# Local transformer: second norm centred on TensorE, PSUM banks and engine orders laid out anew; mixture of experts: routing in groups, gates spread by DMA

## The reference, cut to what matters

```
def attn_layer(x, Wqkv, qs, ksc, Wo):
    q, k, v = jnp.split(x @ Wqkv, 3, -1)
    q = l2norm(q) * qs          # l2norm(t) = t / max(norm(t), 1e-12)
    k = l2norm(k) * ksc
    q, k = rotary with scale (q * cos * scale + rotate_half(q) * sin * scale; k with 1/scale)
    out = local_attention(q, k, v)      # softmax over this window and the one before
    return out @ Wo

def ffn_layer(x, g, bln, W1, b1, W2, b2):
    xn = (x - mean) / jnp.sqrt(var + 1e-05) * g + bln
    a, gate = jnp.split(xn @ W1 + b1, 2, -1)
    return a * jax.nn.gelu(gate, approximate=False) @ W2 + b2

for i in range(6):
    x = attn_layer(shift_tokens(x), ...) + x
    x = ffn_layer(shift_tokens(x), ...) + x
```

```
logits = xf @ router_w + router_b
gates = softmax over the two largest logits, 0 elsewhere     # first index wins a tie
out = sum_e gates[:, e] * (silu(xf @ w1[e]) * (xf @ w3[e]) @ w2[e]) + the same, ungated, of 2 shared experts
```

## Time and profile before

| | |
|---|---|
| median of 3 runs | 6157.06 us |
| the profiled execution | 6155.58 us, its span 6153.5 us |
| PE busy | 5219.1 us, 85% of the span |
| VectorE busy | 4318.1 us, 70% |
| ScalarE busy | 3341.5 us, 54% |
| GpSimd busy | 2611.7 us, 42% |
| mean granted TensorE clock | 0.937 of full speed |
| local transformer | about 1460 to 5295 us of the span |
| mixture of experts | about 5694 to 5963 us of the span |

### The profile page before, as it was taken

One profiled execution on the slowest core, in us unless ns is written; L12 is line 12 of the kernel. 1 busy time (PEld: TensorE's weight loads), 2 busy tenths in 40 slices (PEclk: granted clock), 3 DMA queues, 4 the chain that ended last, 5 costly groups with the idle time before them and its releaser, 6 DMA issues. The chain is left out here.

```text
span 6153.5 us, 131444 instructions
## 1 busy us (share of the span) xinstructions
PE 5219.1 (85%) x50625; PEld 3447.1 (56%) x50817; DVE 4318.1 (70%) x6996; ACT 3341.5 (54%) x5697; POOL 2611.7 (42%) x1602
## 2 busy tenths in 40 slices
...
GB/s 70 55 55 55 18 0 6 2 2 26 11 10 10 28 10 10 10 25 15 10 10 25 15 10 10 25 15 10 10 25 13 11 11 10 11 2 2 7 14 17
DMA packets 74175, 105.08 MB, mean 17 GB/s; under 512 B 21576, under 2 KB 52504, under 8 KB 71072
## 3 DMA queue, kind: packets, MB, share of 16 engines
...
HBM read 61.19 MB, written 2.36 MB: 10 GB/s over the span
## 5 line engine op out<-in xcount | busy, mean ns | idle before, releaser
L2180 POOL TENSOR_TENSOR lt_qk<-lt_qk,lt_rot 128x1024 f32<-128x1024 f32 x384 | 905.2, 2357 | 512.2 <-DVE lt_rot L2534 512.2
L2190 POOL TENSOR_TENSOR lt_prob<-lt_prob,lt_total 128x1024 f32<-128x1024 f32 x192 | 365.3, 1902 | 1238.0 <-DVE lt_total L2560 1231.9
L2229 PE MATMUL lt_ps<-lt_w_qk,lt_xs 128*128 128x512 f32 x1536 | 759.9, 618 | 53.4 <-issue 31.8
L2185 POOL TENSOR_TENSOR lt_qk<-lt_qk,lt_rnorm 128x1024 f32<-128x1024 f32 x384 | 727.9, 1907 | 57.1 <-ACT lt_rnorm L2408 49.5
L2280 PE MATMUL lt_ps<-lt_z,lt_fold 128*128 128x256 f32 x3072 | 678.8, 379 | 1.2 <-ACT lt_z L2436 1.2
L2401 ACT ACTIVATE lt_sq<-lt_ps 128x1024 f32<-128x1024 f32 x384 | 393.4, 1025 | 480.8 <-PE lt_ps L2229 472.4
L2280 PEld LDWEIGHTS lt_ps<-lt_z,lt_fold 128*128 128x128 f32 x3072 | 583.6, 190 | 121.4 <-ACT lt_z L2436 24.3
L2531 DVE TENSOR_TENSOR lt_qk<-lt_ps,lt_table 128x1024 f32<-128x1024 f32 x384 | 466.1, 1214 | 156.2 <-ACT lt_sq L2401 151.9
L2534 DVE TENSOR_TENSOR lt_rot<-lt_ps,lt_table 128x512 f32<-128x512 f32 x768 | 488.9, 675 | 0.0
L2541 DVE TENSOR_REDUCE lt_norm<-lt_sq 128x16 f32<-128x1024 f32 x384 | 463.8, 1208 | 0.0
L2550 DVE TENSOR_REDUCE lt_nmax<-lt_ps 128x16 f32<-128x1024 f32 x192 | 235.1, 1225 | 308.7 <-PE lt_ps L2248 308.4
...
## 6 DMA issues: line engine op xcount, KB each, us to landing
mb_bs<-mb_rows SPq DMA_DIRECT2D x16, 1536.0 KB, 7.6
lt_xw<-lt_xw SPq DMA_DIRECT2D x192, 128.0 KB
mb_bs<-mb_rows SPq DMA_DIRECT2D x16, 512.0 KB, 4.3
...
lt_wvT<-in_L_wvT SPq DMA_DIRECT2D x6, 512.0 KB, 7.2
lt_wo<-in_L_ffn_Wo SPq DMA_DIRECT2D x6, 512.0 KB, 8.4
```

The lines of the kernel that those rows point to most:

```text
L2180: pool.tensor_tensor(qk[:, u, :, :], qk[:, u, :, :], rot[:, u % 2, :, :], ALU.add).then_inc(sg["added"], 1)
L2185: pool.tensor_tensor(qk[:, u, :, :], qk[:, u, :, :], rnorm[:, u, :, :].to_broadcast([P, H, DH]), ALU.mult).then_inc(sg["qk"], 1)
L2229: last = pe.matmul(AT[u][:, 512 * k:512 * k + 512], xs[:, m.j, c:c + P], w_qk[:, a, 512 * k:512 * k + 512], start=True, stop=True)
```

## The change

In the local transformer: `floor` leaves DVE; its work is done on ACT by a Relu of the sum less 1e-24, and the Ln's bias adds it back. The mean is no longer taken and subtracted: one product with `center_w` (identity less 1/128) writes the centred values to PSUM, where ACT's square and DVE's multiplication read them. DVE writes y plus attention output straight to xs2, in two operations of 64 partitions, and so ACT's two copies go; `ffn_out` adds from xs2. g and bln are folded into w_1 and the biases once per layer (`raw_1`, `raw_v`, `b_up`), which takes one multiplication per item from DVE. Each product has new banks, X0 to X3, and the bodies of all engines have a new order. In the mixture of experts: the router works on four groups of two items; the choices of groups 1 to 3 are made by DVE a few operations at a time between the experts' steps; the gates go to DRAM and back by DMA, each row spread over 64 partitions, and the spreading product goes; the shared pair comes first; PE looks two steps ahead; all 40 steps are written out.

```diff
@@ local transformer, ACT
             def inverse_norm(m, u):
+                act.wait_ge(sg["sumsq"], 4 * m.n + u + 1)
+                nc.scalar.activation(log[:, u, :], norm[:, u, :], ACT.Relu, bias=least[:, 0:1]).then_inc(sg["floor"], 1)
                 act.wait_ge(sg["floor"], 4 * m.n + u + 1)
-                nc.scalar.activation(log[:, u, :], norm[:, u, :], ACT.Ln, scale=4.0 ** LIFT).then_inc(sg["ln_norm"], 1)
+                nc.scalar.activation(log[:, u, :], log[:, u, :], ACT.Ln, scale=4.0 ** LIFT, bias=least[:, 1:2]).then_inc(sg["ln_norm"], 1)
...
-            def ffn_tokens(n):
...
@@ local transformer, DVE
-            def floor(m, u):
-                dve.wait_ge(sg["sumsq"], 4 * m.n + u + 1)
-                nc.vector.tensor_scalar(norm[:, u, :], norm[:, u, :], 1e-24, None, ALU.max).then_inc(sg["floor"], 1)
...
             def attended(n):
                 dve.wait_ge(sg["attn_out"], n.n + 1)
-                nc.vector.tensor_tensor(y_of(n), y_of(n), D[:, 0:S], ALU.add).then_inc(sg["y_attn"], 1)
-            def center(n):
...
+                nc.vector.tensor_tensor(xs2[0:64, 0:S], y_of(n)[0:64, :], attn[0:64, :], ALU.add)
+                nc.vector.tensor_tensor(xs2[64:P, 1:S + 1], y_of(n)[64:P, :], attn[64:P, :], ALU.add).then_inc(sg["xs2"], 1)
             def normed(n):
-                nc.vector.tensor_tensor(xn[:, :], cen[:, :], rstd[:, :], ALU.mult).then_inc(sg["xn0"], 1)
-                nc.vector.tensor_scalar(xn[:, :], xn[:, :], vecs[:, 0:1], vecs[:, 1:2], ALU.mult, ALU.add).then_inc(sg["xn"], 1)
+                nc.vector.tensor_tensor(xn[:, :], cen, rstd[:, :], ALU.mult).then_inc(sg["xn"], 1)
...
                 if m:
-                    softmax(m, 0, A)
-                if n:
-                    normed(n)
-                if m:
+                    softmax(m, 0, X2)
+                if n:
+                    hidden(n)
+                if m:
                     sums(m, 0)
-                    softmax(m, 1, C)
+                    softmax(m, 1, X2)
                 if n:
-                    hidden(n)
                     ffn_out(n)
@@ local transformer, PE
-            def mean(n):
-                pe.matmul(Bb[:, 0:S], core.mean_w[:, :], xs2[:, :], start=True, stop=True).then_inc(sg["f_mean"], 1)
+            def centre(n):
+                pe.matmul(cen, core.center_w[:, :], xs2[:, 0:S], start=True, stop=True).then_inc(sg["f_centered"], 1)
...
             def next_layer(l, back, front):
+                pe.wait_ge(sg["raw_in"], 16 * RAW * (l + 1))
+                for k in range(2):
+                    for t in range(FT):
+                        last = pe.matmul(X0[0:frows[t], 512 + k * FT + t:513 + k * FT + t], raw_1[:, c:c + frows[t]], raw_v[:, 1:2], start=True, stop=True)
+                last.then_inc(sg["b_made"], 1)
+                pe.wait_ge(sg["b_up"], l + 1)
@@ mixture of experts, SP
+            for i in range(items):
+                sp.wait_ge(sg["gateT"], i + 1)
+                sp.dma_start(rows[i:i + 1, :].rearrange("a (x w) -> (a x) w", x=E), gatesT[:, i, :]).then_inc(sg["rows"], 16)
+                sp.wait_ge(sg["rows"], 16 * (i + 1))
+                if i >= 3:
+                    sp.wait_ge(sg["hid"], GATED * (i - 2))
+                for k in range(2):
+                    sp.dma_start(gate_b[64 * k:64 * k + 64, i % 3, :, :].rearrange("p e w -> p (e w)"),
+                                 rows[i:i + 1, k * GATED * W:(k + 1) * GATED * W].to_broadcast([64, GATED * W])).then_inc(sg[f"gates{i % 3}"], 16)
@@ mixture of experts, PE
+            logits(0)
+            logits(1)
+            for i in range(EACH):
+                turn(i)
+            logits(2)
+            logits(3)
+            up(0)
+            up(1)
+            for q in range(STEPS):
+                for i in turns(q):
+                    turn(i)
+                if q + 2 < STEPS:
+                    up(q + 2)
+                down(q)
```

More of the change, by code:

```diff
@@ L2391, in _ @@
         def _(act):
-            for name, each in (("square", 4), ("rnorm", 4), ("ln_norm", 4), ("qkT", 4), ("exp", 2), ("pT", 2), ("xw", 1), ("z", 4), ("xs2", 1),
+            for name, each in (("square", 4), ("floor", 4), ("rnorm", 4), ("ln_norm", 4), ("qkT", 4), ("exp", 2), ("pT", 2), ("xw", 1), ("z", 4),
                                ("f_square", 1), ("f_log", 1), ("f_var", 1), ("gelu", 1)):
@@ L3021, in stage_moe @@
         ln = AdaNorm(core, ctx, sg, 2, SHIFT_B, SCALE_B)
+        items = B // 2
+        EACH = items // GROUPS
+        TT = EACH * W // P
         wr = sb("wr", [P, E])
@@ L3111, in _, with turn @@
-            items_loop(pe, items, item)
+            def turn(i):
+                pe.wait_ge(sg["gate"], i // EACH + 1)
+                pe.wait_ge(sg["logit_read"], 2 if i < EACH else GROUPS)
+                if i >= 2:
+                    pe.wait_ge(sg["gateT"], i - 1)
+                for t in range(W // P):
+                    last = pe.transpose(ps_r[0:E, i % 2, t * P:(t + 1) * P], gate[:, i // EACH, (i % EACH) * (W // P) + t, :], core.ident[:, :])
+                last.then_inc(sg["gate_turned"], 1)
@@ L3178, in _ @@
[L3178 to L3190 removed]
+            dve.wait_ge(sg["w_in"], 16 * LOADS)
```

502 lines of the change are left out of this document (273 added, 229 removed).

## The result

The changed kernel takes 5673.93 us, the median of 4 runs (5666.57 to 5680.2), against 6158.2 before, here the median of four runs; the ratio is 0.9213, 95% interval 0.9197 to 0.9229. The forecast was 5808 with a range of 5715 to 5915: the direction was right, the gain was 484 us instead of 350, and the time lies outside the range. Some 110 to 120 of the 134 us of the miss are in the local transformer.

The account below looks back on a forecast made before the run. PE was taken to lead with no engine full, the new body limited by PE's work with waits and a softmax ring; 6155.6 - 249 (bodies) + 5 (layer ends) - 105 (experts) = 5806.6, median 5808 us, range 5715 to 5915.

Parts of the forecast that it names:

- PE's waits without a ring: Local transformer, norm's chain: the new order cuts PE's waits from 4.6 to about 1.0 us, a body of 34.8.
- the floor of any order: Local transformer: a body that never waited on PE would be 33.8 us, the least an order can give.
- The rival of 34.0: Local transformer: PE never waits, both limits looser, 34.0 us a body, 5648 us in all; chance 0.12.
- The ring through the softmax: Local transformer: dependency loop across bodies, scores 0 to next scores 0, sum 33.3, with some 12 handovers 35.1 us.
- Two limits this close add something: Local transformer: PE's work with waits and the ring, nearly equal, delay each other by 0.6 us, making 35.7 a body.
- The size of the start: Local transformer: the old body taken as 38.3 us, from one body, project to project.
- The floor: Local transformer: moving floor's four operations off DVE returns about 4 us a body there, but shortens PE's waits only in part.
- the rest of the gain has to come from the new order: Local transformer: without the floor operations PE's first wait goes in part; the new order must bring the remaining gain.
- The slower rival: Local transformer: hidden waits for a late gelu; from 3.3 us beyond its 2 us slack, 39.6 a body, 6181; chance 0.05.
- Layer ends: Local transformer, six places counting the first: net 0.9 us more each from folding products and small DVE operations, +5 us.
- Mixture of experts: Experts' stage: steps begin at about 17.5 us, 40 steps of 2.8 us, 140 against 245 before, -105 us.
- the 7.3 that the prediction set beside it: Experts' gate loads: the skill's estimate for 1 MB, 7.3 us instead of 5.5, three later groups late by about 1 each.

Follow-up runs that it names:

- max_once: Changed kernel with the maximum taken for t = 0 only, the softmax for t = 1 subtracting it too: 5642.2 us, body 34.06 us.
- ring_short: Changed kernel with one more GpSimd operation of 0.4 us ahead of normalize for t = 1: 5686.2 us, body 34.51 us.
- ring_long: Changed kernel with 1.2 us more of GpSimd work ahead of normalize for t = 1: 5748.8 us, body 35.35 us.
- the five edits in other places: Changed kernel, separately: transposes divided, ACT copy moved earlier, down-projection cut, turn_p 0 sent to X3, that plus divided transposes; body 34.41 us each time.
- fill_3_4: Changed kernel with the transposes of turn_qk 1 divided round centre and var to fill PE's two waits: 5692.4 us, body 34.41 us.
- moe_alone: Kernel before the change with only the new mixture of experts: 6042.8 us, ratio 0.9809 to before.

## Why the prediction was wrong, point by point

- **PE's waits without a ring.** Forecast 34.8, "waits fall to about 1.0". Measured 0.75 in waits and 33.3 of busy PE; with the ring loosened (max_once) the body is 34.06, so this step erred by 0.7. The 33.8 that I called the floor of any order was the body less its marked waits, 38.3 - 4.6, and PE's busy time in such a body, 33.7, agrees with it; it is that busy time which fell to 33.3. No run shows why. A part is likely how ends are modelled: a group ahead of a wait is counted to its modelled end (in after, turn_p 0 counts 1.04 and the next group starts after 0.88), and there are fewer such groups now. The rival of 34.0 ("PE never waits") had the same fault: max_once is at 34.06 with 0.75 of waits left.
- **The ring through the softmax** is the step that failed. Forecast 33.3 and "some 12 handovers" of 0.15, 35.1. By ring_short and ring_long it is 33.99. Two errors make the 1.1: the terms as listed add to 33.0 and not 33.3, and beyond them the ring holds 1.0 where the 12 handovers were to bring 1.8. Groups that follow one another on PE start before the modelled end of the last (attend counts 7.07, the next begins after 6.90), and on DVE likewise (1.23 busy, 1.14 from start to start), which takes back a part of each handover.
- **"Two limits this close add something", 0.6.** They add nothing. Waits and durations repeat to 0.02 us, and the body is the longest ring and no more: the five edits in other places moved it by 0.00, and in ring_short two rings 0.10 apart gave the longer one's 34.51. This 0.6 and the 1.1 of the ring, less the 0.42 by which another ring is longer, are the 1.3 between 35.7 and 34.41, and 95 x 1.3 = 123 us. The local transformer missed by 110 in the traces (forecast -244, measured -354), because its layer ends and last layer gained less than plain bodies.
- **Which ring** was not the one forecast either: it closes by the reuse of a PSUM pair (X1, rotate 0) and DVE's written order, not by the data from normalize to turn_p 1, though the two differ by only 0.42. From scores 0 to turn_p 1 are 14.9 us, from there to turn_qk 0, behind attend, 13.4, and on to scores 0 6.1. Such a sum gives 34.4 on every closed path of a loop, with its slack; what shows which path is tight is the edit that moves the body.
- **The size of the start.** 38.3 was one body; the mean was 38.48, with the bodies at a lower clock.
- **The floor.** Right that alone it gives little (0.3 forecast and, at full clock, measured; 0.41 in the mean). Its weight shows in the new order only, 2.05 at full clock and 2.7 in the mean, so "the rest of the gain has to come from the new order" was half of it: order and floor need each other. That its four cost DVE "about 4 us a body" was right in the sum (4.0), though one of the four took 0.26 and three 1.1 to 1.3.
- **The slower rival** (hidden late) was placed rightly and priced too low: hidden late by 4 costs 6.5, since the clock falls behind the wait. In the changed kernel hidden follows the softmax for t = 0 without a wait, so gelu was in time.
- **Layer ends.** Forecast +0.9 each. The two distances around one (36.70 and 45.38, before 38.30 and 50.86, at the first) exceed two plain bodies by 12.9 on the average of the five ends, and before by 10.8 (two of 38.48): +2.1. Not foreseen: in the last layer, whose loop stands in the program a second time, PE idles without a releaser ("issue"), 22 us in after and 10 in before, and its bodies are 36.8 on average against 39.6, a gain of 2.8 instead of 4. Of after, the waits and then the instruction loads (count, MB) of the same 500 us:

```profile
PE lt_ps L2259 <- issue: 12.4, 11, 2.2
PE lt_ps L2240 <- issue: 9.7, 3, 3.3
```

```profile
q8 instruction: 33, 0.54, 0.5%
```

In 2170 to 2580 us, inside the second layer, there is not one such load. Each of the ten waits above 1 us ends 1.4 to 1.7 us behind the end of a load, and fill_3_4, whose last layer is 12 us longer, has 58 loads in the same 500 us. So these waits are for instructions; why one copy of the loop needs the loads and the other doesn't isn't shown.

- **Mixture of experts.** Forecast -105, measured -117 in the traces, -122 in moe_alone. Head 17.0 us from the first logits, against 17.5. A step 2.58 and not 2.8: at full clock a product follows another by 0.86, where the earlier trace rows gave 0.94 as the half of a pair's busy time, the same error as with the handovers. The gate loads of 512 KB each landed in 5.7 us as a median (4.6 to 5.0 the first of a pair, 6.4 to 6.7 the second), and both of an item were in 6.9 to 7.2 us behind the first's issue, where I took 5.5; the 7.3 that the prediction set beside it was the better figure, and so was its consequence: DVE waited for them 1.7 us in all, three times.
